# PE's head loop written out, expert loads moved ahead of the next head's weights, and two half projections moved in PE's order

## The reference, cut to what matters

```python
mixed = hidden_states @ w_qkv                    # 256 -> 16*128 + 16*128 + 32*128
z = (hidden_states @ w_z).reshape(B, S, HV, DV)
y = conv1d(mixed, conv_w)                        # 4 taps, each channel by itself
q, k, v = split(silu(y));  q, k = l2norm(q), l2norm(k)
def step(Sm, inp):                               # over the 512 tokens, for each of 32 value heads
    Sm = Sm * exp(g_)
    delta = (v_ - k_ @ Sm) * b_
    Sm = Sm + outer(k_, delta)
    return Sm, q_ @ Sm
on = rmsnorm(o * silu(z)) * norm_w
x = x + on @ w_out + experts(xn)
```

## Time and profile before

| | us |
|---|---|
| median of 3 runs | 3381.91 (3374.16 to 3387.66) |
| the profiled execution, its own time | 3380.46 |
| its span | 3378.6 |
| PE busy | 2890.9 (86%) |
| DVE busy | 2420.4 (72%) |
| ACT busy | 1765.5 (52%) |
| POOL busy | 1193.4 (35%) |

### The profile page before, as it was taken

How to read it: one execution, slowest core, us unless ns; L and a number is a source line. 1 busy time by engine, 2 the same in 40 slices (tenths; PEclk the granted TensorE clock), 3 DMA queues, 4 the chain that set the end, 5 groups by cost and what they waited for, 6 DMA issues and landing times. The chain is left out here.

```text
span 3378.6 us, 131146 instructions
## 1 busy us (share of the span) xinstructions
PE 2890.9 (86%) x52588; PEld 2392.8 (71%) x52588; DVE 2420.4 (72%) x5194; ACT 1765.5 (52%) x5613; POOL 1193.4 (35%) x1120
## 2 busy tenths in 40 slices
PE   2698989898989899898989898989898989827778
PEld 1577877777777777787878787878787878614445
DVE  7477777777777767676867676777777767368886
ACT  1365556565655656565656565656565656401111
POOL 4444444444232323232323232323233333253320
PEclk7799999999999989898989899989899989958889
DMA  4211111110111110101010101110101010351110
GB/s 155 80 55 51 44 44 35 40 33 28 31 38 31 38 31 24 43 23 45 23 45 23 45 23 45 23 45 23 45 23 45 23 45 22 93 171 56 57 31 13
DMA packets 95378, 151.62 MB, mean 45 GB/s; under 512 B 17323, under 2 KB 65026, under 8 KB 94064
## 3 DMA queue, kind: packets, MB, share of 16 engines
q1 hardware_dynamic: 70928, 108.05, 10.8%
q0 software_dynamic: 12288, 24.19, 2.3%
q10 hardware_dynamic: 11520, 10.49, 0.9%
HBM read 110.84 MB, written 41.22 MB: 45 GB/s over the span
## 5 line engine op out<-in xcount | busy, mean ns | idle before, releaser
L1250 DVE SCALAR_TENSOR_TENSOR p_y<-p_xr,p_cw,p_y 128x512 f32<-128x512 f32 x768 | 680.0, 891 | 111.3 <-ACT p_y L1003 92.8
L1061 ACT ACTIVATE p_Xs<-p_psI 128x256 f32<-128x256 f32 (+1 forms) x386 | 161.5, 418 | 657.3 <-PE p_psI L749 475.0
L705 PE MATMUL p_psF<-xnS,p_w_hl 128*128 128x512 f32 x1536 | 429.0, 424 | 72.4 <-issue 51.0
L1470 POOL TENSOR_TENSOR p_E<-p_E,p_sj 128x512 f32<-128x512 f32 x128 | 130.6, 1041 | 833.6 <-DVE p_sj L1275 833.6
L705 PEld LDWEIGHTS p_psF<-xnS,p_w_hl 128*128 128x128 f32 x1536 | 291.3, 200 | 134.9 <-issue 53.2
L1293 DVE TENSOR_TENSOR p_ATP<-p_psF,p_E 128x512 f32<-128x512 f32 x256 | 165.3, 686 | 254.7 <-PE p_psF L736 238.1
L1478 POOL TENSOR_TENSOR p_M<-p_ATc,p_masks 128x512 f32<-128x512 f32 x128 | 169.9, 1332 | 378.7 <-ACT p_ATc L1041 365.5
L749 PEld LDWEIGHTS p_psI<-p_Dc,p_M 32*32 32x32 f32 x16384 | 177.6, 109 | 145.8 <-issue 141.2
L749 PE MATMUL p_psI<-p_Dc,p_M 32*32 32x32 f32 x16384 | 207.7, 198 | 75.5 <-DVE p_DTc L1311 56.0
L717 PE MATMUL p_psF<-p_w_hl,xnS 128*128 128x256 f32 x1536 | 257.1, 323 | 14.9 <-issue 14.8
L870 PE MATMUL p_psO<-p_wout,p_ont 128*128 128x256 f32 x1056 | 256.4, 399 | 0.6 <-ACT p_zs L1019 0.6
(11 more groups left out here) (309 smaller groups left out, 6607.0 us busy)
## 6 DMA issues: line engine op xcount, KB each, us to landing
p_ab<-decays SPq DMA_DIRECT2D x64, 512.0 KB, 5.3
p_w_raw<-in_w_in SPq DMA_DIRECT2D x17, 768.0 KB, 4.0
expert_out<-p_ye ACTq DMA_DIRECT2D x80, 128.0 KB, 1.7
p_wgu<-in_w_gu SPq DMA_DIRECT2D x56, 176.0 KB
expert_in<-p_zero SPq DMA_DIRECT2D x16, 512.0 KB, 9.7
p_xe<-expert_in SPq DMA_DIRECT2D x56, 128.0 KB
p_wd<-in_w_down SPq DMA_DIRECT2D x56, 88.0 KB
p_wout<-in_w_out SPq DMA_DIRECT2D x16, 256.0 KB, 2.6
```

The costliest lines, as they stand in the source:

```text
L705: m = pe.matmul(b4(psF[f % 2][:, :]), w_hl[:, wp, kt, ty * P:(ty + 1) * P], xnS[:, xp, kt, :].rearrange("p (b t) -> p b t", b=B)[:, :, c * ...
L1061: act.activation(dst, src, ACT.Copy).then_inc(s["xs" if l < 5 else "join_xs"], 1)
L1250: m = dve.scalar_tensor_tensor(y[:, ty, :, :], xr[:, ty, :, tap:tap + P], cw[:, ty, tap:tap + 1], y[:, ty, :, :], ALU.mult, ALU.add)
```

## The change

PE's loop becomes a Python loop, so its 16 passes stand one behind another and its waits are against constants. ACT, DVE and POOL keep their loops. SP issues the expert's three loads before `w_raw` and `cw_raw` in chunk 0. In chunk 1 `project_out` is split: batches 0 and 1 stay, batches 2 and 3 go behind `level5_y`; DVE's `gather_out` goes behind the scans there. In chunk 0 the third of z's four batches goes from behind `level_y(3)` to ahead of `level_x(3)`.

```diff
@@ sync, step
                 sp.dma_start(ab[:, :, :, :].rearrange("p v b t -> p v (b t)"),
                              adram[bass.ds(2 * kh, 2), c, :].partition_broadcast(P)).then_inc(s["ab_in", p], 16)
-                if c == 0:
-
-                    sp.wait_ge(w_split, kh * 3 + 3)
-                    sp.dma_start(w_raw[:, :, :], w_row(kh + 1)).then_inc(w_in, 16)
-                    sp.dma_start(cw_raw[:, :, :], taps_row(kh + 1)).then_inc(w_in, 16)
                 wait_place(sp, "filled", kh, c, EX_DOWN, ago=2)
...
+                if c == 0:
+
+                    sp.wait_ge(w_split, kh * 3 + 3)
+                    sp.dma_start(w_raw[:, :, :], w_row(kh + 1)).then_inc(w_in, 16)
+                    sp.dma_start(cw_raw[:, :, :], taps_row(kh + 1)).then_inc(w_in, 16)
@@ tensor
-            def project_z(kh, c, half):
-
+            def project_z(kh, c, batches):
+
+                half = batches[0] // 2
                 f = Z1 if half else Z0
-                slot_free(kh, c, f)
-                if c == 0:
-                    pe.wait_ge(w_split, kh * 3 + 3)
-                for b in (2 * half, 2 * half + 1):
+                if batches[0] % 2 == 0:
+                    slot_free(kh, c, f)
+                    if c == 0:
+                        pe.wait_ge(w_split, kh * 3 + 3)
+                for b in batches:
...
-                m.then_inc(s["filled"], 1)
+                if batches[-1] % 2:
+                    m.then_inc(s["filled"], 1)
@@ tensor, step
-                project_out(kh, c - 2, (0, 1, 2, 3))
+                project_out(kh, c - 2, (0, 1) if c == 1 else (0, 1, 2, 3))
...
                 level5_y(kh, c - 1)
+                if c == 1:
+                    project_out(kh, c - 2, (2, 3))
...
                 state_update(kh, c - 1)
+                if c == 0:
+                    project_z(kh, c, (2,))
                 level_x(kh, c, 3)
                 expert(kh, c, EX_DOWN)
                 level_y(kh, c, 3)
-                project_z(kh, c, 1)
+                project_z(kh, c, (2, 3) if c else (3,))
...
-            with heads_loop(nc, "heads_pe", mybir.EngineType.PE, HK) as (kh, announce):
+            for kh in range(HK):
                 for c in range(NC):
-                    if c == NC - 1:
-                        announce()
                     step(kh, c)
@@ vector, step
                 conv(kh, c, 1)
-                gather_out(kh, c - 2)
+                if c != 1:
+                    gather_out(kh, c - 2)
                 decays(kh, c, 0)
                 decays(kh, c, 1)
+                if c == 1:
+                    gather_out(kh, c - 2)
                 key_scales(kh, c)
```

More of the change, by code:

```diff
@@ L910, in step @@
                 turn(kh, c, QUERIES_T, lambda b: kq[c % 2][:, b, Q_, :], "silu", 2)
-                project_z(kh, c, 0)
+                project_z(kh, c, (0, 1))
                 solve(kh, c - 1)
```

## The result

The changed kernel takes 3230.47 us (median of 4 runs, 3227.31 to 3237.65) against 3378.03 us before (4 runs, 3360.32 to 3387.66). The ratio is 0.957 with a 95% interval of 0.953 to 0.962: 147.6 us less, where 163 were forecast. The time lies in the stated range, 11 us above the predicted 3219.

What follows compares the result with a forecast made beforehand. PE, busy for 86% of the span, sets the pace, so its idle time and clock count. -108 - 20 - 35 + 0 = -163 us from 3380.46 gives 3217, stated as 3219 for the median; range 3165 to 3285.

Steps and rivals of the forecast that it cites:

- The edge of a pass: Start of each pass: PE's branch, the loads' DMA wait and half clock go, 7.2 us per edge, -108 us.
- the first two terms of the sum: -108 us for the edge of a pass and -20 us for other issue stalls.
- if only the branch goes: Smaller bound of the edge's gain: 3.4 us of branch at 15 edges, 51 us.
- Other stalls of issue: Inside PE's levels: with code written out, packet borders move, mostly into long matmuls; -20 of 32.1 us.
- Chunk 1: project_out in two halves: same length at full clock, but better clock, 2.2 us in 16 passes, -35 us.
- Lost 1.4, regained 1.4: 0: Chunk 0's moved z ahead of level_x(3) waits for ACT's copy, fills no gap: 0, bounds -8 and +14 us.
- DVE taking the edge over: Rival at the start of a pass: DVE's own loop return delays PE, 56 us come back, 3275 us; chance 0.17.
- The clock holding nearly everywhere: Rival: chunk 1 gives 59 us, the edges 126, the issue stalls 30, so 3167 us; chance 0.13.
- Slower code fetch in straight code: Rival: each 16 KB packet in the passes stalls PE; at 0.5 us a packet 3418 us; chance 0.04.

Runs made afterwards that it cites:

- e6: Kernel before with PE's loop written out and the expert's loads first, without the moved halves: 3261.94 us, ratio 0.969.
- e1: Kernel before with PE's loop written out and nothing else: 3491.19 us against 3467.93 on that chip, ratio 1.007.
- e7: Kernel before with the expert's loads first, PE's loop kept and its branch hint moved ahead of chunk 3's last level: 3322.32 us, ratio 0.987.
- e5: Changed kernel run again unaltered, on a second chip: 3230.88 us, ratio 0.960 to the kernel before.
- e10: Changed kernel with DVE's gather_out behind the key scales in chunk 1: 3208.14 us, ratio 0.952 to the kernel before.
- e9: Changed kernel with ACT's copy of the up matmul earlier in chunk 0: 3223.12 us, ratio 0.955 to the kernel before.
- e11: Changed kernel with the edits of e8, e9 and e10 together: 3184.19 us, ratio 0.944 to the kernel before.
- e2: Kernel before with the expert's loads issued ahead of the next head's weights and nothing else: 3424.61 us, ratio 0.988.
- e12: Kernel before with 128 empty instructions written into PE's loop body; the program that ran had one register move more per pass instead: 3375.74 us, one run.
- e3: Changed kernel with chunk 0's z whole again in its old place: 3328.88 us, ratio 0.960 to the kernel before.
- e4: Changed kernel with chunk 1's project_out in one piece and gather_out in its old place: 3341.38 us, ratio 0.964 to the kernel before.
- e8: Changed kernel with DVE's loop written out too: 3216.77 us, ratio 0.955 to the kernel before.

## Why the prediction was right, and where it was not

**The edge of a pass: right in mechanism and size.** Forecast -108 us; e6 has the edge without the moved halves and measured -110. Writing out the loop also moves the stalls of issue, so e6 holds the first two terms of the sum, -128 together; they missed by 18. The steps hold one by one: products 0 came 7.8 us earlier in pass 8 where 8.4 were worked out, the difference being mostly the wait for ACT, 0.75 us instead of 0.4. What the prediction did not say is that its two parts don't add. It gave 51 us as the bound "if only the branch goes"; e1 shows that the branch alone gives nothing and loses 0.7%, because the loads' arrival is fixed by POOL's last part of the weights and not by PE. The two waits stand in a row with the DMA behind, so the first can only be cashed in when the second is gone.

The Trainium skill ("Runtime: NRT & Kernel Launch", instruction fetch mechanics) says that kernels prefer full unrolling because of the branch's fetch. With the loads first the time agrees (0.969 in e6 against 0.987 in e7, where PE's loop stands); alone, in e1, it does not.

**Other stalls of issue: wrong.** The step "between nothing and all of 32.1 I take -20 us" failed, and so did its reason, that most borders will fall in stretches of long matmuls. Before, issue in L749, L758 and L717 comes to 61.5 us in 72 stalls (14.6, 32.1 and 14.8); changed, L752, L761 and L719 have 63.8 in 69 (8.4, 49.9 and 5.5). The stalls did move to other places in each pass, as forecast, but did not get fewer to speak of, nor shorter. Nor do they simply grow as PE gets faster: e5 has 66.2 us, e10 66.8, e9 81.2 and e11 83.0, and in passes 4 to 14 the two profiles of the changed kernel alone differ by 8.6 (39.0 and 47.6).

That they are packets of code arriving late was only argued in the prediction. The traces bear it out. The changed kernel's trace has 107085 instructions of PE (matmuls, weight loads and waits) and 418 packets of its queue, 256 instructions to a packet. Counted from the first instruction, all 69 stalls stand at place 191 or 192 of a run of 256, and in each of them PE goes on 1.2 to 1.6 us after a packet of that queue has landed; where PE passes the same place without a stall, the packet had landed 3.1 us before in the median. One of them, whose packet landed at 1467.33:

```profile
1468.65 0.26 PE L761 MATMUL p_psI<-p_Xs,p_DTc 32*32 32x32 f32 x8 [1.08 <-issue]
```

The second profile of the same kernel (e5) has its 69 at the same two places. In the kernel before, with its loop, a stall comes behind the 1431st, the 2301st and the 3045th matmul of a pass in each of passes 4 to 14, and so it does in e2 and e7, on two different chips; in e12, with its one instruction more, they come behind the 1430th, 2300th and 3044th, again in each. What makes a packet late at 69 borders and not at the others stays open. Stalls of another kind are in the first four passes of e1, e3 and e4, all on one chip: 56 to 59 in each, at other places of the 256; what those are is open too.

**Chunk 1: right in mechanism, size off.** The wait ahead of the gate matmul was forecast as 1.2 us and measured as 18.5 us in 16, its longest 1.2; the new wait for the keys was forecast too. PE's timeline in chunk 1 of pass 8 shows both, then the stretches of this chunk in pass 8 and pass 14:

```profile
1485.59 0.63 PE L729 MATMUL p_psF<-ident,p_kq 128*128 128x128 f32 x4 [0.66 <-ACT p_kq L1018]
...
1493.94 0.67 PE L888 MATMUL p_psF<-p_xeT,p_wgu 128*88 128x128 f32 x4 [1.18 <-DVE p_ATP L1298]
```
```profile
1479.14:1515.87 36.73, 34.80 (x789) 29.23 (x781) 28.21 (x56) 23.59 (x78) 11.77 (x11) 1.00 0.14 38
2454.69:2492.85 38.16, 35.15 (x789) 29.40 (x781) 29.58 (x60) 24.94 (x80) 11.77 (x11) 1.00 0.18 41
```

Both run at a clock of 1.00. Pass 14's 38.16 us are 0.2 more than the 37.95 before, so at full clock the chunk is as long as it was; pass 8's is the shortest of the 11. Full clock is what the chunk was forecast to gain, 2.2 us a pass, and over passes 4 to 14 it went from 40.81 us at 0.925 to 38.62 at 0.989, 2.2 less. But that is not the split's alone: without either moved half (e6) it is 40.30 at 0.937, without the split alone (e4) 39.38 at 0.962, without z's move alone (e3) 38.78 at 0.992. The term was -35 us; e4 gives some 21 for the split as the last of the edits. e10 shows that the reading was right to the end: the wait was gather_out's new place holding back the key scales, and moving it away won another 1.1 us a pass.

**Chunk 0's piece of z: the step "Lost 1.4, regained 1.4: 0" was mis-sized.** The 2 us wait for p_usb is there as forecast (26.7 us in 16, 2.1 at the longest), but e3 shows 0.8 us a pass of gain, 13 us. The bound I gave on that side was 8. What the step left out is what the clock of chunk 0 gains: its mean is 0.952 with the move and 0.931 without. The clock withheld comes to 2.0 us and 2.9 us a pass (41.44 x 0.048 and 42.27 x 0.069), a difference of 0.9, as large as the gain. The rest of the chunk is as long with the move as without, 39.5 and 39.4 us, as forecast.

**The sum.** -110 (edge), about -21 (chunk 1) and -13 (z) make -144, and -147.6 was measured, -141 in e5. On e5's chip alone it is -110 (e6) and -31 for the two halves together, where -128 and -35 were forecast: the 18 are nearly the stall term of 20, which did not come (73.3 us of issue in e6). Within the halves 14 too many in chunk 1 were nearly made up by 13 in z that were taken as 0; that part of the agreement is luck.

**The rivals.** DVE taking the edge over had 0.17; e8 rules it out in the steady passes. Its premise, that the cover shrinks, was right: in the timeline of DVE the convolution now starts with an idle time of 0.33 us. The clock holding nearly everywhere (0.13) came half true: 0.98 in passes 4 to 14, 0.989 in chunk 1 but 0.952 in chunk 0. Slower code fetch in straight code would have needed over 200 us of issue in the levels and has 63.8, and the same stalls stand in the kernel with its loop; e1's loss would have looked like it, and only its waits show that it was the DMA.

## What to carry to other kernels

When two waits stand in a row on one engine and the second has an outside clock (a DMA that another engine releases), removing the first alone only lengthens the second; work out when the second would be ready with the first gone, before adding up. Moving work into a gap fills it only if the work's own wait is over by then: look for what releases its buffer, on the other engine's order. And where the engine that waits is TensorE, count the half clock after an idle time with it. A stall that stands at the same instruction in every pass, with nothing waited for, is to be laid beside the packets of the engine's instruction queue before a gain is put on it.

## What the runs showed that I had not expected

- Writing out the loop of the engine that bounds the kernel made it slower by itself, ratio 1.007 (1.005 to 1.009), and was worth 1.9% on top of the other edit (0.988 to 0.969).
- A branch hint some 290 instructions ahead of PE's branch left the median at 3246 ns, with 3278 before. ACT's, DVE's and POOL's branches are recorded with 49 to 68 ns.
- Issue stalls in PE's levels and z stayed at 61.5 us before and 63.8 changed, and are 81 with e9's edit (61.5, 13.4 and 6.3) and 83 in e11. In the changed kernel all 69 stand at one place of every 256 instructions.
- The four passes with POOL's scatter took about 183 to 200 us each on one chip and 164 to 182 on the others, while passes 4 to 14 of e2 and e7, which differ only in the hint, agree between the two chips (1858.18 and 1857.57 us).
